# Graph attention in a four-layer graph and feed-forward network: one exponential per score, counts as logarithms, skip products between the heads

## The reference, cut to what matters

```python
xl = (x @ W).reshape(n, heads, out_ch)
alpha_src = jnp.einsum('nhc,hc->nh', xl, a_src)
alpha_dst = jnp.einsum('nhc,hc->nh', xl, a_dst)
e = jax.nn.leaky_relu(alpha_src[src] + alpha_dst[dst], 0.2)
m = jax.ops.segment_max(e, dst, num_segments=n)
e = jnp.exp(e - m[dst])
s = jax.ops.segment_sum(e, dst, num_segments=n)
alpha = e / (s[dst] + 1e-16)
out = jax.ops.segment_sum(xl[src] * alpha[:, :, None], dst, num_segments=n)
```

## Time and profile before

| | us |
|---|---|
| median of 3 runs | 1560.32 (1554.13 to 1561.17) |
| the profiled execution | 1560.62 |
| its span, first to last instruction | 1558.8 |
| TensorE busy in the span | 1389.7 (89%) |
| VectorE, ScalarE, GpSimd busy | 1004.3, 768.8, 321.4 |
| granted TensorE clock, mean | 0.93 of 2.4 GHz |

### The profile page before, as it was taken

How to read it: one execution, slowest core, us unless ns; L and a number is a source line. 1 busy time by engine, 2 the same in 40 slices (tenths; PEclk the granted TensorE clock), 3 DMA queues, 4 the chain that set the end, 5 groups by cost and what they waited for, 6 DMA issues and landing times.

```text
span 1558.8 us, 24036 instructions
## 1 busy us (share of the span) xinstructions
PE 1389.7 (89%) x9990; PEld 1178.2 (76%) x9990; DVE 1004.3 (64%) x1828; ACT 768.8 (49%) x1191; POOL 321.4 (21%) x159
## 2 busy tenths in 40 slices
PE   6999999799999798888796999569899999958798
PEld 5999533699433795678686999459799999958786
DVE  8645777545777657465575674846577777768555
ACT  2345887335887353354534454434345554425433
POOL 3000776000766200125361004021000000010100
PEclk8999999899999897999997899789899999976899
DMA  8165363146352140234106453052355555060200
GB/s 325 54 211 176 123 180 90 61 134 206 102 177 82 61 157 7 92 129 146 61 22 235 144 178 143 21 193 76 138 182 183 183 184 185 28 253 1 71 1 21
DMA packets 31123, 195.52 MB, mean 125 GB/s; under 512 B 4243, under 2 KB 4372, under 8 KB 15015
## 3 DMA queue, kind: packets, MB, share of 16 engines
q1 hardware_dynamic: 31014, 193.98, 36.7%
HBM read 183.74 MB, written 3.93 MB: 120 GB/s over the span
## 4 chain that ended last, share of the span: by engine, by line
PE 70%; DVE 17%; ACT 6%; POOL 5%; issue 2%; DMA 1%; SPq 0%; DVEq 0%; POOLq 0%
PE PS L358 54%; PE PS L919 5%; PE PS L928 5%; PE PS L363 3%; POOL WL L308 2%; POOL WK L1107 2%; DVE WK L1678 2%; PE PS L455 1%; PE PS L603 1%; DVE WK L1699 1%; DVE WL L301 1%; ACT GS L476 1%; DVE SM L1246 1%; DVE GS L480 1%; DVE XS L480 1%
## 5 line engine op out<-in xcount | busy, mean ns | idle before, releaser
L358 PE MATMUL PS<-XS,WH 128*128 128x256 f32 x2436 | 447.9, 287 | 14.5 <-DVE XS L480 11.0
L294 ACT ACTIVATE WH<-w 128x768 fp32r<-128x768 f32 x381 | 316.8, 841 | 287.2 <-PE PS L358 278.2
L301 DVE TENSOR_TENSOR WL<-w,WH 128x768 fp32r<-128x768 f32 x315 | 300.2, 961 | 195.8 <-ACT WH L294 193.1
L358 PEld LDWEIGHTS PS<-XS,WH 128*128 128x128 f32 x2436 | 385.0, 195 | 18.8 <-issue 11.0
L358 PE MATMUL PS<-XS,WL 128*128 128x256 f32 x1218 | 347.2, 285 | 0.0
L358 PEld LDWEIGHTS PS<-XS,WL 128*128 128x128 f32 x1218 | 236.6, 194 | 0.0
L1107 POOL TENSOR_TENSOR WK<-WK 128x1024 f32<-128x1024 f32 x64 | 152.9, 2392 | 266.2 <-ACT WK L992 266.2
L1049 DVE TENSOR_TENSOR WK<-PS,WK 128x1024 f32<-128x1024 f32 x128 | 156.5, 1223 | 57.4 <-ACT PS L995 56.4
L308 POOL TENSOR_TENSOR WL<-w,WH 128x768 fp32r<-128x768 f32 x66 | 125.4, 1917 | 321.2 <-ACT WH L294 321.2
L358 PE MATMUL PS<-WH,GS 128*128 128x256 f32 x864 | 162.8, 287 | 6.8 <-DVE GS L480 6.7
L995 ACT ACTIVATE PS<-PS 128x1024 f32<-128x1024 f32 x128 | 129.3, 1010 | 34.6 <-PE PS L919 34.5
(11 more groups left out here) (239 smaller groups left out, 2010.8 us busy)
## 6 DMA issues: line engine op xcount, KB each, us to landing
w<-f2W_in SPq DMA_DIRECT2D x40, 1152.0 KB, 5.4
w<-Wrel_in SPq DMA_DIRECT2D x12, 1152.0 KB, 8.3
WK<-qrep_in SPq DMA_DIRECT2D x16, 768.0 KB, 5.5
w<-f1Wi_in SPq DMA_DIRECT2D x8, 1152.0 KB, 6.2
w<-f1Wo_in SPq DMA_DIRECT2D x8, 1152.0 KB, 5.1
w<-f3Wqkv_in SPq DMA_DIRECT2D x6, 1152.0 KB, 15.5
RT<-qg_rows SPq DMA_DIRECT2D x16, 384.0 KB, 6.4
RT<-AS SPq DMA_DIRECT2D x32, 192.0 KB, 6.7
```

The costliest lines, as they stand in the source:

```text
L294: A.e.activation(w_hi(i), w_raw(i), ACT.Copy).then_inc(*hi("w", i))
L301: V.e.tensor_tensor(w_lo(i), w_raw(i), w_hi(i), ALU.subtract).then_inc(*lo("w", i))
L358: ins = T.e.matmul(o, l, r, start=i == 0 and first, stop=i == n - 1 and last, skip_group_check=lint)
```

## The change

Everything below is one edit.

- **Dots from PSUM.** `pe_gemm_N` gets a bank for every 256 columns (`wide=256`), and VectorE takes the dot products of each bank as soon as it is there; ScalarE alone copies xl to SBUF after them.
- **One exponential.** Up to a term that is the same for all sources, leaky_relu(s + d) is max(s + 0.8 d, 0.2 s). ScalarE makes the rows 0.2 s from PSUM (`low_rows`), VectorE adds and takes the maximum (`scores`), then adds the logarithm of the count and takes the extreme value (`with_logs`), and ScalarE computes a single exponential whose accumulator is the sum (`accum_out`).
- **Logarithms.** GpSimd and ScalarE prepare `LOGS` and `LOGS1` once, in the L0 block (`logs_counts`); they replace `Cn`, `NM`, `C1`, `NM1`.
- **Order of the heads.** `rows`, `head`, `soft`, `turn_p`, `agg`, `leave` go head by head, with fixed PSUM banks (`bank_at`); ScalarE makes all copies of the turned weights.
- **Single heads by halves.** The layers with one head treat the two halves of the nodes apart (`one_rows`, `one_turn`, `one_agg`, `one_leave`), with the steps placed between the slices of a skip product in L1 (`between`).
- **Skip products between the heads.** Seven of the eight tiles of the L1 skip product stand between steps of the heads, the eighth behind the transposes of the norm; the second skip product is one unit before and two units after the sum of the single head.
- **Subtracts.** The lower parts of all 48 tiles of L1's and L2's attention weights move from GpSimd to VectorE.
- **L1's rows for x** are loaded early and added by GpSimd right after the norm, half by half. **L2** turns its first four heads' output before the last head's sum. **L3** multiplies the attention vectors into the weights first (`VB`), gets scores and rows from products, and the features follow after the first rows. The warm-up products in front of L1's inner norm go.

The core of it, common indentation taken off and most removed lines left out (they are in the listing above):

```diff
     ("f0om", "f0Wom", None, 12, "V"), ("f0w1", "f0W12", None, 6, "V"),
-    ("g1W1", "g1W1", None, 8, "G"), ("g1Wr1", "g1Wr1", None, 8, "G"),
-    ("g1W2", "g1W2", None, 8, "G"), ("g1Wr2", "g1Wr2", None, 8, "G")]
+    ("g1W1", "g1W1", None, 8, "V"), ("g1Wr1", "g1Wr1", None, 8, "V"),
...
     main.append(("f1dn7", "f1Wo", 7, 3, "V"))
-    main += [("g2W1", "g2W1", None, 8, "G"), ("g2W2", "g2W2", None, 8, "G")]
...
     aggregate(2, XSv)
+    if n == "1":
+        A.wait_ge(pool, "counts")
+        A.e.activation(Cn, Cn, ACT.Ln).then_inc(*act())
+        A.e.activation(LD, LD, ACT.Ln).then_inc(*act("logs"))
...
+def logs_counts():
+    G.wait_ge(vec, "Cn")
+    G.wait_ge(pe, "ah", 2)
+    G.wait_ge(cols_in, "cols")
+    G.e.tensor_scalar(LOGS[:, :], Cn, 0.0, BIG, ALU.is_equal, ALU.mult).then_inc(*pool())
+    G.e.tensor_scalar(off, ident, 0.0, None, ALU.is_equal).then_inc(*pool())
+    for m in range(2):
+        G.e.tensor_tensor(LD3[:, m, :], Cn3[:, m, m * P:(m + 1) * P], ident, ALU.add).then_inc(*pool())
+    G.wait_ge(pool)
+    for m in range(2):
+        G.e.tensor_tensor(LE3[:, m, :], L3[:, m, m * P:(m + 1) * P], off, ALU.mult).then_inc(*pool())
+    G.e.tensor_scalar(LD, LD, 1.0, None, ALU.max).then_inc(*pool())
+    G.e.tensor_scalar(Cn, Cn, 1.0, None, ALU.max).then_inc(*pool("counts"))
+    G.wait_ge(act, "logs")
+    G.e.tensor_tensor(LOGS[:, :], LOGS[:, :], Cn, ALU.add).then_inc(*pool())
+    G.wait_ge(pool)
+    G.e.tensor_copy(LOGS1[:, :], LOGS[:, :]).then_inc(*pool())
+    G.wait_ge(pool)
+    for m in range(2):
+        G.e.tensor_tensor(L13[:, m, m * P:(m + 1) * P], LD3[:, m, :], LE3[:, m, :], ALU.add).then_inc(*pool())
+    pool.also("logs")
...
+    def rows(h0):
+        b = bank_at(h0 // 2 % 2, (n + "as", h0), (vec, n + "z", h0 + 1))
+        for h in (h0, h0 + 1):
+            ins = row_of(b[:, (h - h0) * 256:(h - h0 + 1) * 256], h)
+        ins.then_inc(*pe(n + "as", h0))
...
+    def low_rows(h0):
+        A.wait_ge(pe, n + "as", h0)
+        if h0 >= 4:
+            A.wait_ge(vec, n + "z", h0 - 3)
+        A.e.activation(g.B[h0 // 2 % 2], two(ps(n + "as", h0)), ACT.Copy, scale=0.2).then_inc(*act(n + "bs", h0))
     def soft(h):
+        A.wait_ge(vec, n + "z", h)
+        for m in range(2):
+            z = g.Z[h % 3][:, m, :]
+            A.e.activation(z, z, ACT.Exp, bias=g.low[:, m, h:h + 1], scale=-1.0,
+                           accum_out=g.den[:, m, h:h + 1]).then_inc(*act())
+        act.also(n + "exp", h)
...
+    at(-1)
+    for i in range(H + 1):
+        if i < H:
+            soft(i)
+        if i >= 2 and i % 2 == 0 and i + 2 < H:
+            low_rows(i + 2)
+        at(i)
+        if i >= 1:
+            turn_p(i - 1)
...
+def scores(g, as_, b, m, h):
+    z = g.Z[h % 3][:, m, :]
+    V.e.scalar_tensor_tensor(out=z, in0=as_, scalar=g.ad[:, m, h:h + 1], in1=b, op0=ALU.add,
+                             op1=ALU.max).then_inc(*vec())
+def with_logs(g, m, h):
+    z = g.Z[h % 3][:, m, :]
+    return V.e.tensor_tensor_reduce(z, z, g.logs[:, m, :], -1.0, 1.0e20, ALU.add, ALU.min, g.low[:, m, h:h + 1])
...
+    def head(h):
+        V.wait_ge(act, n + "bs", h - h % 2)
+        if h >= 3:
+            V.wait_ge(pe, n + "tp", h - 3)
+        V.wait_ge(vec, n + "dots")
+        V.wait_ge(pool, "logs")
         for m in range(2):
+            scores(g, ps(n + "as", h - h % 2)[:, h % 2 * 256:h % 2 * 256 + 256], g.B[h // 2 % 2][:, h % 2, :], m, h)
         V.wait_ge(vec)
         for m in range(2):
+            with_logs(g, m, h).then_inc(*vec())
+        vec.also(n + "z", h)
+    def leave(h):
         j = h % g.per
+        if j < g.per - 1:
             return
+        for m in range(2):
+            weights_sums(g, m, h - j, h + 1)
+        for m in range(2):
+            V.wait_ge(pe, n + "o", m, h - j)
+            V.wait_ge(vec)
+            evac(m, h - j, h + 1, 0, C, ps(n + "o", m, h - j)[:, 0:g.per * C], g.den[:, m, :])
+            vec.also(n + "o", m, h - j)
+    head(0)
+    for i in range(H + 2):
+        at(i)
+        if i + 1 < H:
+            head(i + 1)
+        if i >= 2:
+            leave(i - 2)
...
+def one_vec(g):
+    n = g.name
+    V.wait_ge(vec)
+    vec.also(n + "rows")
+    for o, a in ((g.asr, g.as3), (g.ad, g.ad3)):
+        V.e.tensor_reduce(o[:, :, 0], a, AX.X, ALU.add).then_inc(*vec())
+    vec.also(n + "dots")
+    V.wait_ge(act, n + "bs")
+    V.wait_ge(vec)
+    V.wait_ge(pool, "logs")
+    for m in range(2):
+        scores(g, ps(n + "as")[:, 0:256], g.B[0][:, 0, :], m, 0)
         V.wait_ge(vec)
+        with_logs(g, m, 0).then_inc(*vec(n + "z", m))
+    V.wait_ge(pe, n + "tp", 1)
+    vec_copy(*half_of(g, 1), n + "pt", 1)
...
 def l1gnn_sync():
+    load_row("g1br2", 768, (vec, "f0v", 512, 1))
+    load_row("g1be2", 768, (pe, "om", 512, 0, 1))
     load_units(w1 + 10)
-    load_row("g1as1", 1024, (vec, "f0v", 512, 1))
-    load_row("g1ad1", 1024, (pe, "om", 512, 0, 1))
-    load_row("g1b1", 1024, (vec, "f0x"))
-    load_units(w2 + 11)
+    load_row("g1as1", 1024, (vec, "f0x"))
+    load_units(w1 + 16)
+    load_row("g1ad1", 1024, (pool, "g1br2"))
+    load_row("g1b1", 1024, (pool, "g1rows"))
+    load_units(w2 + 8)
     load_row("g1as2", 768, (vec, "g1a_rows"))
     load_row("g1ad2", 768, (vec, "g1a_rows"))
-    load_units(wr2 + 11)
-    load_row("g1br2", 768, (vec, "g1a_o", 1, 2, 0))
-    load_row("g1be2", 768, (vec, "g1b_rows"))
-    load_row("g1b2", 768, (vec, "g1b_rows"))
-    load_row("g1g2", 768, (pool, "g1rows"))
+    load_units(wr2 + 8)
+    load_row("g1b2", 768, (vec, "g1a_o", 1, 2))
+    load_row("g1g2", 768, (vec, "g1b_rows"))
...
+    def at(i):
+        if i in (-1, 0, 2, 4):
+            skip(*{-1: (0, 1), 0: (1, 3), 2: (3, 4), 4: (4, 5)}[i])
+    gat_pe(gat1, lambda o, h: as_rows(gat1, o, h), lambda: T.wait_ge(act, "g1xl", 768, 1), at)
+    skip(5, 7)
+    pe_to_T("h1T", g1o, 8, lambda m: T.wait_ge(vec, "g1ln", m), lambda k: [(act, "h1", k)], (0, 1, 2, 3))
+    skip(7, 8)
+    pe_lin8("g1xm", w2, range(3), lambda u, m: (act, "g1xm", u, m), hs_before("h1"), ((4, 5), (6, 7), (0, 1)))
...
+    def between(u, k):
+        if (u, k) == (0, 2):
+            one_rows(gat1b, 4)
+        elif (u, k) == (0, 5):
+            one_turn(gat1b, 0, 5)
+        elif (u, k) == (0, 6):
+            one_turn(gat1b, 1, 4)
+        pe_lin8("g1s", wr2, us, lambda u, m: (vec, "g1s", u, m), hs_before("h1"), ((2, 3), (2, 3), (4, 5)), between)
+    skip2(range(1))
+    T.wait_ge(act, "g1xm", 2, 1)
+    one_agg(gat1b, 0, (6, 7))
+    one_agg(gat1b, 1, (0, 1))
+    skip2(range(1, 3))
+    turn[0] = 0
...
+def xl_vec(g, name, t0, rows_):
+    count = []
+    feed_vec(ahead(t0))
+    for c in range(0, 1024, 256):
+        for m in range(2):
+            xl_dots(g, name, m, c, rows_, count)
+        if c < 768:
+            feed_vec(ahead(t0 + c // 128 + 2))
+    V.wait_ge(vec)
+    vec.also(g.name + "rows")
+    vec.also(g.name + "dots")
...
+    def at(i):
+        if i == -1:
+            xl_out("g1xl", g1xl, 768)
+        elif i in (0, 1, 2, 4):
+            skip(*{0: (0, 2), 1: (2, 3), 2: (3, 4), 4: (4, 5)}[i])
+    gat_act(gat1, at)
+    skip(5, 7)
     act_sqrt("g1ln")
...
     act_sqrt("g1ln")
     for k in range(0, 8, 2):
         A.wait_ge(pe, "h1T", k)
         for i in range(2):
             A.e.activation(h1T[:, k + i, :], two(ps("h1T", k))[:, i, :], ACT.Relu, bias=col("g1be1", k + i, 1),
                            scale=col("g1g1", k + i, 1)).then_inc(*act())
         act.also("h1", k)
+    skip(7, 8)
     for k in range(0, 8, 2):
         A.wait_ge(vec, "h1sum", k)
         act_upper(HSv[:, 0, k:k + 2, :], h1T[:, k:k + 2, :], "h1", k)
...
+            if stat:
+                xstat("f1a", m, u * 256, (u + 1) * 256)
...
     V.wait_ge(*row_sem("g1g2"))
     for m in range(2):
         V.e.scalar_tensor_tensor(out=g1o2[:, m, :], in0=g1o2[:, m, :], scalar=ag[:, m, 0:1],
                                  in1=row("g1g2")[:, 0:768], op0=ALU.subtract, op1=ALU.mult).then_inc(*vec("g1g2", m))
+    V.wait_ge(vec)
+    for m in range(2):
         V.e.scalar_tensor_tensor(out=x3[:, m, :], in0=g1o2[:, m, :], scalar=rr[:, m:m + 1], in1=x3[:, m, :],
                                  op0=ALU.mult, op1=ALU.add).then_inc(*vec("g1x", m))
+    lin8_feed(feed_vec, wr2, [1])
+    for m in range(2):
+        xstat("f1a", m, 0, 256)
+    skip_out(1)
+    lin8_feed(feed_vec, wr2, [2])
+    skip_out(2)
...
 def l1gnn_pool():
-    feed_pool(wr2 + 8)
-    G.wait_ge(vec, "g1s", 2, 1)
     for n in ("g1br2", "g1be2"):
         G.wait_ge(*row_sem(n))
-        G.e.tensor_tensor(x3, x3, bcast2(n), ALU.add).then_inc(*pool())
-        G.wait_ge(pool)
-    pool.also("g1rows")
+        for m in range(2):
+            G.wait_ge(vec, "g1a", m)
+            if n == "g1be2":
+                G.wait_ge(pool, "g1br2", m)
+            G.e.tensor_tensor(x3[:, m, :], x3[:, m, :], row(n)[:, 0:768], ALU.add).then_inc(*pool(n, m))
+        pool.also("g1rows" if n == "g1be2" else n)
...
+    def at(i):
```

(33 more changed lines are left out.)

616 lines of the change are left out of this document (281 added, 335 removed), and 1 row of the table main.

## The result

The changed kernel takes 1504.05 us (median of 4 runs, 1502.14 to 1508.56) where the kernel before took 1560.12 beside it: a ratio of 0.9652, with a 95% interval of 0.962 to 0.9685. The forecast was 1502. The profiled execution has a span of 1500.4 us, against 1558.8. The total was met by luck in part: two of its three large terms were off by 8 and 10 us, and their errors cancelled.

A forecast was written before the change was run, and what follows sets the result against it. TensorE holds 70% of the chain, so gains must come from the three graph attention stages (288 of 1558.8 us), where it is not kept busy. Terms -28 - 23 - 12 + 4.4 = -58.6 gave 1502 us; 8-in-10 range 1484 to 1531.

The forecast's parts named there:

- Stage 1, forecast -28: First graph attention stage: 100.6 us against 129.8, a gain of 29 with 1 given back for VectorE's load.
- four heads with 7 skip tiles: Stage 1, between its two weight products: heads interleaved with skip tiles take 36.8 us against 49.1.
- Stage 2, forecast -23: Second graph attention stage, eight heads without skip tiles: 78.4 us against 101.6, taking 2.6 us a head.
- Stage 3, forecast -12: Third graph attention stage, twelve heads of 64: 45 us against 57, first sum at 11 us.
- I take 2.8: Stage 3's time per head in us, between TensorE's 1.8 at the upper clock and 3.3 at the lower.
- Rival 1: Clock rises, stages 2 and 3 run at 2.4 GHz: stages -29, -27, -22, total 1486 us; chance 0.13.
- Moved subtracts: Stages 1 and 2: 48 tiles add 46 us of VectorE work, claimed hidden; uncovered up to 46 us.
- The tail's rows: Stage 1's tail: POOL waits 9.8 us, adds two rows in 6.9, then the norm's row loads in 4.9; unneeded there.
- Small ones: Logarithms +1.5, feeds in two feed-forward tails +0.9 and +1.5, square root table ahead of stage 3 +0.5: +4.4 us.
- rival 2: Chain inside a head sets the pace, 3.5 us a head: -37, 1523 us; chance 0.30 shared with two other rivals.
- rival 3: Stages 1 and 2: VectorE becomes the bound, a third of 46 us uncovered: -43, 1517 us; 0.30 shared with two others.
- rival 4: Slower: products in stages 1 and 2 fall to 1.2 GHz, all 864 costing 81 us, 1583 us; chance 0.03.

The follow-up runs named there:

- the scores first: Changed kernel with one edit: between stage 1's heads VectorE does the next head's scores before the next skip tile's subtract; 1502.34 us, 0.9627.
- the three orders mended: Changed kernel with scores before the subtract, next weight tile's upper part before the eight activations, root before the evacuation; 1494.98 us, 0.9578.
- features-first run: Changed kernel with one order undone: in stage 3 TensorE makes the features ahead of the first score rows; 1513.59 us, 0.9715.
- second experiment: Changed kernel with one edit: ScalarE writes the next weight tile's upper part before stage 1's eight activations of normed rows; 1497.8 us, 0.9615.
- gap run: The 1482.71 us version (three edits, spare products, three more order changes) plus an unused 104-column tile behind the constants; 1481.26 us, 0.9505.
- the fastest version: Changed kernel with three order edits, spare TensorE products in waits, and three more order changes; 1482.71 us, 0.9514.
- the run with both parts together: Kernel before with the 48 subtracts moved to VectorE and stage 1's two rows loaded and added early by GpSimd; 1549.03 us, 0.9946.

## Why the prediction was right, and where it was wrong

*Stage 1, forecast -28, measured -18.1.* W1 took 17.3 us (its 144 products at the pace of the 162 in the first 19.45 us; forecast 17.7; the late row load cost nothing). **The failed step is "four heads with 7 skip tiles", 36.8 us forecast, 44.8 measured.** Its sum of TensorE's work, 26.8 us to the end of the last skip tile ahead of the norm, left out that the order of two queues ties the engines in a circle of 4.46 us: it ended at 31.5, and at 27.7 with the scores first. I had seen that VectorE was busy 21 of 22 us and gave 1 us back for it; the price was in the order, not in the load. Then the root came 3.4 us behind the statistics, as foreseen (3.6), and from the transposes to W2 it was 10.0 instead of 7.2, since VectorE's first addition stood behind the subtract of a tile that ScalarE had put behind eight activations. W2 took 20.1 (forecast 18.6, the upper end was 20.2), its first 5.3 us at the lower clock behind the wait of 5.88:

```profile
760.20:765.50 5.30, 5.30 (x25) 5.30 (x26) 2.74 (x5) 1.49 (x2) 0.00 (x0) 0.50 0.00 0
```

The single head took 29.6 (27.5), 1.3 of it a wait for a weight tile of the last products. With the three orders mended the stage is 102.8, 2.2 us above the forecast's sum.

*Stage 2, forecast -23, measured -22.1.* This too is a sum of errors that cancel. Start to first sum was near the forecast (25.3 us against 24.4). The heads took 17.0 us instead of 20.8: 1.33 us each where the clock was the upper one and nothing was waited for (966 to 970), and one wait of 2.88 behind the evacuation of four heads, where the forecast had 2.6 for each:

```profile
973.83 0.96 PE L362 MATMUL PS<-cp,WK 128*128 128x128 f32 x4 [2.88 <-ACT WK L1669]
```

The second turn was ready 5.9 us behind the last head (forecast 4.5), and the single head took 16.8 instead of 14.4, its sum 6.7 at a granted clock of 0.79 (forecast 6.2).

*Stage 3, forecast -12, measured -19.9 with its tail, -20.7 to the last sum.* First sum at 13.5 us (forecast 11), then **1.9 a head, where the step "I take 2.8" was mis-sized**. Rival 1 had the size for this stage (-22) and what goes with it: the granted clock is 0.97. The row that I set against it, 1425.2, was read rightly: in the kernel before TensorE is busy without a gap and stays mostly low, with transposes of 1.06 us to the end.

```profile
1424.00:1438.00 14.00, 14.00 (x76) 13.97 (x76) 10.02 (x34) 6.44 (x15) 0.00 (x0) 0.57 0.01 2
```

In the features-first run the same transposes were back at 0.6 us 6 us after a wait of 3.58. Why the kernel before did not come back in 14 us is open; no run here tests it, so that the waits of the old stage kept its clock down is argued, not shown. For stage 2 rival 1's -27 did not come: it still has waits of 3.26 and 2.88. How the gains of these two stages divide among the single exponential, the dots from PSUM and the order of the heads was not run apart.

*Moved subtracts, forecast hidden.* Not hidden, but a gain that I did not price. Alone they are worth 7.4 us in stage 1, most of it since the dots lose GpSimd's hold (6.1 us of waits). In the changed kernel, whose dots read PSUM, they cost 2.9 us between the heads of stage 1 and save 6.4 in W1, where weights would stand behind the early adds; in all they save 2.5 us of stage 1 and 2.8 of stage 2.
The Trainium skill, "SBUF — State Buffer", section "SBUF: two separate sides", excludes GpSimd's operations against VectorE's with two SBUF inputs; the trace agrees: with the subtracts on GpSimd the dots with one operand in PSUM take 421 ns, eight of them while a GpSimd subtract ran, and the additions with both in SBUF 868 ns on average, the three held ones between the heads 1.6 to 2.1 us.

*The tail's rows.* The prediction's first example, 9.8 of waiting, 6.9 of adds and 4.9 of load in the chain, is not 20 us of gain. Alone it is -2.7 in the tail and, with what it costs in W1, +5.3 for the stage; beside the moved subtracts it is nothing. In the changed kernel the wait ahead of the closing transposes is 1.12 us instead of 10.40; the rows or the subtracts account for 2.7 of that, and what gave the rest, the halves of the single head or the skip products behind its sum, was not run alone.

*Small ones, forecast +4.4, measured +1.6.* The tails' feeds are as forecast: waits of 2.68 instead of 1.81 us ahead of stage 1, 1.36 instead of none ahead of stage 2. The logarithms cost nothing that a wait shows (+1.5 forecast), though the same instructions ahead of stage 1 vary by 4 us between traces, so a cost of that size could not be seen. Neither does the table load ahead of stage 3 (0.99 against 1.04). In their place stands a term that nobody had: +4.2 in the second feed-forward stage, of which the gap behind the constants takes back 2.9.

*Rivals.* The chain inside a head (rival 2) sets the pace in stage 1, at 4.46 us with the weight tile's two steps in it, and not in stages 2 and 3. VectorE as a bound (rival 3) is half of that circle. The products did not fall to the lower clock as a whole (rival 4): W1 of both stages ran at 1.00, and W2 of stage 1 was low for its first 5.3 us.
The Trainium skill, "TensorE: Matmul & The Clock Gate", section "HAM oscillation — how this bites in real kernels", has an engine that waits again and again between short groups of products start each of them throttled. The runs agree behind waits of 3.58 and 5.88 us, with 5 to 6 us at the lower clock each, and not behind the 2.06 us ahead of W2 with its weight tile early, where the products ran at 1.00. Behind the same wait of 3.32 us the transposes of stage 1 ran at 1.00 in the changed kernel and at 0.71 in the second experiment. The changed kernel has too few long waits for the picture as a whole.

## What to carry to other kernels

Where two engines hand work to each other in fixed orders, add up the circle (here exponential, upper part of a weight tile, its subtract, scores: 4.46 us) and not only each engine's load; a line moved in one queue was worth 3.4 us and three of them 9. A chain's rows are no price list: before a part is given the time it holds in the chain, ask which other part already takes it. Judge an edit of a few us by the stage's own windows in two traces, with the granted clock beside them, since the same instructions outside it differ by more. And when a total comes out as forecast, compare the terms: here 10 us too little in one stage and 8 too much in another met the sum.

## What the runs showed of the hardware that was not expected

- **The operands' place changes TensorE's pace.** With the constants 608 bytes longer, the same products at a granted clock of 1.00 go at 171 in 20 us instead of 173 (1.1%); moved on by 416 bytes more they are back at 173. The four kernels with the old place take 318.4 to 319.4 us for the second feed-forward stage, the nine with the new 322.0 to 323.8. The gap run changes nothing else, so the place is the cause; which of the moved tiles does it was not tried.
- **The clock gives and takes without a change in the program.** The instructions ahead of stage 1 are the same in eight of the traces and take 698.0 to 702.2 us; those behind stage 3 take 109.7 to 114.7 us in seven. The mean granted clock of the whole is 0.930 before and 0.957 after, and 0.969 in the fastest version.
- **A tiny operation can be held as well.** VectorE's 128x2 addition in the tail of stage 1 took 3.00 us beside GpSimd's row add (timeline of the moved subtracts alone); without GpSimd's adds there, in the run with both parts together, it takes 0.15.

```profile
801.94 3.00 DVE L1735 TENSOR_SCALAR SM<-SM 128x2 f32<-128x2 f32 x1
```
